# Second attention of a one-core kernel: narrow products and selection issued in batches of eight instead of four

## The reference

```python
qh = q.reshape(B, h, dq, Lq)     # 32 batches, 8 heads, 8 channels, 256 queries
kh = k.reshape(B, h, dq, Lk)     # 256 keys
vh = v.reshape(B, h, dv, Lk)
qk = jnp.einsum('bhdq,bhdl->bhql', qh, kh) * scale
sm = jax.nn.softmax(qk, axis=-1)
ret = jnp.einsum('bhql,bhdl->bhdq', sm, vh)
```

## Time and profile before

| what | value |
|---|---|
| median of 3 runs | 817.76 us |
| profiled execution, first to last instruction (span) | 814.5 us |
| TensorE busy | 755.2 us (93%) |
| VectorE busy | 513.3 us (63%) |
| ScalarE busy | 435.3 us (53%) |
| stage of the change, from the first st to the last `products` | about 270.9 to 520.2 us |
| mean granted TensorE clock | 0.975 |

### The profile page before, as it was taken

How to read it: one execution, slowest core, us unless ns; L and a number is a source line. 1 busy time by engine, 2 the same in 40 slices (tenths; PEclk the granted TensorE clock), 3 DMA queues, 4 the chain that set the end, 5 groups by cost and what they waited for, 6 DMA issues and landing times. The chain is left out here.

```text
span 814.5 us, 16953 instructions
## 1 busy us (share of the span) xinstructions
PE 755.2 (93%) x5377; PEld 576.9 (71%) x5377; DVE 513.3 (63%) x871; ACT 435.3 (53%) x862; POOL 295.0 (36%) x354
## 2 busy tenths in 40 slices
PE   4788889999995999999999999689999999999997
PEld 3677667888985666666666666367787778878776
DVE  3888857897797877887788787462344244253222
ACT  3888834344442777778777787633322332233221
POOL 3455542224446524433533443153222223213222
PEclk9999979999996899999999999889999999999999
DMA  5444410000004433433333331000000000000000
GB/s 146 119 112 128 116 59 1 1 0 0 1 21 127 131 99 97 113 109 94 110 106 100 94 112 44 1 1 1 1 1 27 1 1 26 0 0 0 27 1 27
DMA packets 48093, 43.88 MB, mean 54 GB/s; under 512 B 7860, under 2 KB 46356, under 8 KB 48052
## 3 DMA queue, kind: packets, MB, share of 16 engines
q1 hardware_dynamic: 45892, 37.46, 16.2%
q0 software_dynamic: 2160, 5.90, 2.6%
HBM read 27.99 MB, written 15.07 MB: 53 GB/s over the span
## 5 line engine op out<-in xcount | busy, mean ns | idle before, releaser
L1321 DVE TENSOR_REDUCE a_smax<-a_s 128x4 f32<-128x1024 f32 x128 | 154.4, 1209 | 46.6 <-PE a_s L1255 46.4
L1155 ACT ACTIVATE a_prob<-a_st 128x512 f32<-128x512 f32 x256 | 144.6, 591 | 34.9 <-PE a_st L1243 33.8
L1593 POOL TENSOR_TENSOR f_hs_lo<-f_hid,f_hs_hi 128x512 fp32r<-128x512 f32 (+1 forms) x56 | 73.3, 1308 | 197.4 <-ACT f_hs_hi L1539 197.4
L1243 PE MATMUL a_st<-qop,kop 128*128 128x256 f32 x512 | 120.7, 318 | 1.0 <-DMA qop<-a_neg_t 0.6
L1243 PEld LDWEIGHTS a_st<-qop,kop 128*128 128x128 f32 x512 | 77.2, 189 | 60.3 <-ACT a_prob L1155 44.2
L117 PE MATMUL f_bank<-wd_hi,f_hs_hi 128*128 128x256 f32 (+1 forms) x352 | 104.4, 297 | 7.2 <-POOL f_hs_lo L800 6.2
L1653 DVE TENSOR_TENSOR f_prod<-f_sg,f_bank 128x512 f32<-128x512 f32 x44 | 30.2, 687 | 128.1 <-PE f_bank L119 110.4
L1539 ACT ACTIVATE f_hs_hi<-f_hid 128x512 fp32r<-128x512 f32 (+1 forms) x56 | 35.4, 632 | 139.4 <-PE f_bank L119 99.8
L1255 PE MATMUL a_s<-kop,qop 127*128 127x256 f32 x512 | 104.9, 291 | 4.9 <-DVE a_smax L1321 2.6
L119 PE MATMUL f_bank<-wd_hi,f_hs_lo 128*128 128x256 f32 (+1 forms) x352 | 99.3, 282 | 0.0
L118 PE MATMUL f_bank<-wd_lo,f_hs_hi 128*128 128x256 f32 (+1 forms) x352 | 99.0, 281 | 0.0
(11 more groups left out here) (180 smaller groups left out, 1393.0 us busy)
## 6 DMA issues: line engine op xcount, KB each, us to landing
kop<-kop_rows SPq DMA_DIRECT2D x128, 48.0 KB
qop<-qop_rows SPq DMA_DIRECT2D x128, 48.0 KB
kop_rows<-k_hi SPq DMA_DIRECT2D x32, 128.0 KB, 2.3
qop_rows<-q_hi POOLq DMA_DIRECT2D x30, 128.0 KB, 2.6
x_all<-in_x SPq DMA_DIRECT2D x4, 512.0 KB, 4.7
ctx_t<-in_ctx SPq DMA_DIRECT2D x16, 128.0 KB, 2.0
kop_rows<-k_lo SPq DMA_DIRECT2D x16, 128.0 KB, 2.3
a_ctx<-in_ctx SPq DMA_DIRECT2D x16, 128.0 KB, 2.1
```

What stands on the lines that cost most here:

```text
L1155: act.activation(prob[:, u % 8], st_ps[u % 2][:], ACT.Exp, scale=SCALE1).then_inc(prob_ready, 1)
L1243: mm = pe.matmul(st_ps[u % 2][:, c * D:(c + 1) * D], lhsT=kop[t.slot][:, u // 4, c * P:(c + 1) * P], rhs=qop[t.slot][:, u // 4, u % 4], st ...
L1321: dve.tensor_reduce(smax[:, v.slot, 2 * j:2 * j + 2].rearrange("p u q -> p (u q)"), s_ps[j % 2][:].rearrange("p u (q n) -> p (u q) n", q=2 ...
L1593: pool.tensor_tensor(hs[1][0:r, c % 2], hid[0:r, c % 2], raw(hs[0][0:r, c % 2]), ALU.subtract).then_inc(hs_ready, 1)
```

## The change

`products` loses its argument c and issues both halves of the keys in one go, which makes eight products in place of four, or 16 instructions. `selected` likewise loses m and issues both parts together. The places in the unit loop change with it: the last quad of tile o at u = 2, behind `turn`, in place of u = 1 and 3; the first three quads of tile t at u = 6, 10 and 14 in place of 5 and 7, 9 and 11, 13 and 15; the selection at u = 7 in place of 6 and 8. The waits are the same ones, ahead of the whole batch. The number of products and what they compute stay as they are, and no other engine's program changes.

```diff
--- before.py
+++ after.py
@@ -1196,38 +1196,36 @@
                             mm = pe.transpose(misc[0:HALF, q * P:(q + 1) * P], raw(neg[:, h, q]), ident[:])
                         mm.then_inc(neg_done, 1)
 
-                def products(w_, q, c):
+                def products(w_, q):
 
                     if not w_.inside(TILES):
                         return
-                    if c == 0:
-                        after(pe, prob_ready, w_, UNITS, 4 * q + 4)
-                        after(pe, vt_ready, w_)
-                        if q:
-                            after(pe, pv_ready, w_, QUADS, q)
-                        else:
-                            after(pe, pv_ready, w_.plus(-1), QUADS)
-                    for v4 in range(4):
-                        u = 4 * q + v4
-                        mm = pe.matmul(pv_ps[v4 * 32:(v4 + 1) * 32, 0:D], lhsT=vt[:, w_.slot, c, u],
-                                       rhs=prob[:, u % 8, c * D:(c + 1) * D], start=(c == 0), stop=(c == DC - 1),
-                                       tile_position=(0, v4 * 32))
-                    if c == DC - 1:
-                        mm.then_inc(pv_done, 1)
-
-                def selected(w_, m):
+                    after(pe, prob_ready, w_, UNITS, 4 * q + 4)
+                    after(pe, vt_ready, w_)
+                    if q:
+                        after(pe, pv_ready, w_, QUADS, q)
+                    else:
+                        after(pe, pv_ready, w_.plus(-1), QUADS)
+                    for c in range(DC):
+                        for v4 in range(4):
+                            u = 4 * q + v4
+                            mm = pe.matmul(pv_ps[v4 * 32:(v4 + 1) * 32, 0:D], lhsT=vt[:, w_.slot, c, u],
+                                           rhs=prob[:, u % 8, c * D:(c + 1) * D], start=(c == 0), stop=(c == DC - 1),
+                                           tile_position=(0, v4 * 32))
+                    mm.then_inc(pv_done, 1)
+
+                def selected(w_):
 
                     if not w_.inside(TILES):
                         return
-                    if m == 0:
-                        after(pe, pv_ready, w_, QUADS)
-                        if t.inside(TILES):
-                            after(pe, neg_t_ready, t, 2)
-                    for q in range(QUADS):
-                        mm = pe.matmul(misc[q * 32:(q + 1) * 32, m * D:(m + 1) * D], lhsT=(sel_out, sel_den)[m][:],
-                                       rhs=pv[:, w_.slot, q], start=True, stop=True, tile_position=(0, q * 32))
-                    if m == 1:
-                        mm.then_inc(sel_done, 1)
+                    after(pe, pv_ready, w_, QUADS)
+                    if t.inside(TILES):
+                        after(pe, neg_t_ready, t, 2)
+                    for m in range(2):
+                        for q in range(QUADS):
+                            mm = pe.matmul(misc[q * 32:(q + 1) * 32, m * D:(m + 1) * D], lhsT=(sel_out, sel_den)[m][:],
+                                           rhs=pv[:, w_.slot, q], start=True, stop=True, tile_position=(0, q * 32))
+                    mm.then_inc(sel_done, 1)
 
                 for u in range(UNITS):
                     j, k = divmod(u, 2)
@@ -1258,12 +1256,12 @@
                             mm.then_inc(s_done, 1)
                     if u == 2:
                         turn(t, 1, lambda: after(pe, vt_ready, t))
-                    if u in (1, 3):
-                        products(o, 3, u // 2)
-                    if u % 2 and u > 3:
-                        products(t, u // 4 - 1, u % 4 // 2)
-                    if u in (6, 8):
-                        selected(o, u // 2 - 3)
+                    if u == 2:
+                        products(o, 3)
+                    if u in (6, 10, 14):
+                        products(t, (u - 6) // 4)
+                    if u == 7:
+                        selected(o)
                     if u == 11:
                         def before():
                             after(pe, neg_t_ready, t, 2)
```

## The result

The changed kernel takes 825.99 us (median of 4 runs, 824.92 to 827.43) against 817.76 before: a ratio of 1.0102, 95% interval 1.0086 to 1.0119. It is slower by 8.2 us where 10.3 were forecast. Its profiled execution has a span of 824.4 us, for which the sum had said 824.8.

What follows compares the result with a forecast made beforehand. TensorE's own order bounds the kernel: a 15.83 us step less 1.67 saved, plus 0.05 for `turn` and 2.21 of waits, gives 16.42. With both end tiles that adds 10.3 us to 817.8, so 828 us, range 811 to 834.

Steps and rivals of the forecast that it cites:

- the sum: Whole stage: 8.3 us from fourteen full steps, 0.5 from the first tile, 1.5 from the last, 10.3 slower in all.
- TensorE's order as the bound before: Kernel before: TensorE's own order fills the 15.83 us step; ScalarE and VectorE have some 3 us of slack.
- The saving of a merge: TensorE's batches: each merged pair saves 0.33 us, five pairs a step save 1.67 us.
- The waits for the exponential: Runs between batches: st waits for ScalarE's exponential of two units before, delays of 0.50, 0.23, 0.64 and 0.67 us.
- The walk: One changed step followed with durations from the earlier trace: 2.21 us of waits, a 16.42 us step; chance 0.66.
- The loop of 1.19 us: Two st buffers: from a run's first st through its exponential to the third st's weight load takes 1.19 us.
- One sign that the prediction named: Changed trace: st weight loads wait for exponentials at units 5, 6, 10, 14, 1 and 2, 0.25 to 0.6 us each.
- The late `turn`: Unit 2: VectorE's negation lets `turn` go at 2.74 where TensorE comes at 2.57, a delay of 0.17 us.
- The end of the stage: Last tile, without s: exponentials hold it more, four units take 3.4 us; +1.5 us, between 0 and 2.5.
- Rival 1: Faster: the exponentials' loop doesn't close and batches cover the rest; 793 us without waits, 809 at the lower bound; chance 0.14.
- Rival 2: No change: waits without bare loads or late `turn`, 1.34 us a step; 815.3 to 820.2 us; chance 0.10.
- Rival 3: VectorE takes over: bunched reductions make s wait in two runs, 0.3 us each; 836 us; chance 0.10.

Runs made afterwards that it cites:

- half reductions: Changed kernel with each VectorE maximum over 128 of the 256 keys: 824.15 us, ratio 1.0083 against the kernel before.
- half exponentials: Changed kernel with ScalarE's exponentials over 256 of the 512 columns: 821.18 us, ratio 1.0045 against the kernel before.
- moved copies: Changed kernel with ScalarE's quad copies one unit earlier: all four 822.81 us, ratio 1.0077; three of them 822.30 us, ratio 1.0063, against the kernel before.

## Why the prediction was right

**TensorE's order as the bound before: right.** Halving both other engines' work moved the kernel before by 0.07% (interval 0.9983 to 1.0003).

**The saving of a merge, 0.33 us: right.** One merge gave 0.33, two 0.65. The Trainium skill's rule that a change of the tiling mode drains the TensorE (TensorEngine Tiling (Array Packing), Tiling Modes, Key Properties) agrees in sign; that the whole 0.33 us is this drain was not tried.

**The waits for the exponential: right in kind, place and nearly in size.** The walk had units 3 to 6 last 3.61 us and units 8 to 10 2.86, from the first st of the run to the first st of the next; the trace has 3.63 and 2.86. In units 11 to 14 the walk had st 14 at 2.27 behind st 11; it is at 2.25 in one step and at 2.19 in the next. In units 15 to 2 it had st 1 at 1.35 and st 2 at 2.09; they are at 1.30 and 2.06. A step came to 16.19 for 16.42, which makes the waits 16.19 - 14.21 = 1.98 us for 2.21. The loop of 1.19 us, found in the first tile, is the 1.20 of units 3 to 5 after the change. Two spacings of the walk, 0.48 and 0.49 behind an exponential, don't follow from the lines of the earlier trace rows to which it points, but the trace before has them: its exponential at 362.37 is followed by the copy at 362.86.

One sign that the prediction named doesn't tell the kernels apart: weight loads of st that wait for an exponential are as frequent in the kernel before (see the half reductions).

**The late `turn`, 0.17: wrong.** The walk let TensorE come to `turn` 2.57 us behind the first st of the run and the negation release it at 2.74. Its products start at 2.64, which is 0.58 behind st 2 and the pace without a wait: 0.34 behind a bare load and 0.24, where the walk had counted 0.48. With half reductions, where the negation ends 0.7 us earlier, they start at 2.64 as well. The negation took 0.34 or 0.35 us in this place, not the 0.52 of the earlier trace rows. But the margin is next to nothing: the weight load of `turn` starts 0.12 behind the negation's end, at 2.57 in one step and at 2.63 in the next. So as soon as the waits for ScalarE shrink, by half exponentials or by moved copies, s and `turn` wait for VectorE, and `turn` the more as the negation, beside GpSimd's addition, then takes 0.52 to 0.57.

**The sum: two errors that cancel in part.** Counted as the sum counts, from the first st of a tile, the first tile gave 0.4 us for 0.5, the 14 full steps 5.0 for 8.3, and the last tile 2.7 for 1.5. A full step grew by 0.36 us where the walk had 0.59. The end of the stage was undersized: four units in the last tile take the 3.4 us that the walk said, but its distance to before was cut down to 1.5 where the trace has 2.7 (first st of the tile to the last batch: 512.25 to 527.83 after, 506.27 to 519.15 before).

**The rivals.** Rival 1 (no wait, pure gain) is what the two halved engines give in part, 0.90 of 1.6 us a step; in the kernel as it is ScalarE's waits stand, and VectorE's behind them. Rival 2 is refused by the interval. Rival 3, VectorE in charge, is refused for the changed kernel by the halved reductions, and is what comes right behind. No branch of the forecast had that: rival 1 let the loop of the exponentials open and left VectorE out, but with half exponentials alone the step was still 15.80 us. The chance given to "faster" would have needed both to vanish.

## What to carry to other kernels

A merge that saves time on the busiest engine also takes away the gaps in which the others caught up. Before merging, take from the trace how long a double buffer's loop is (here 1.19 us from one st to the second next) and how much work fits between: merge as long as the runs left between batches don't exceed it. Here two units fit between two batches, so two merges of five brought 1.05%, and all five cost 1.0%; a run of three lost 0.23 to 0.30 us, about what one merge brings. Where a run is one unit too long, move independent work of the same engine into it; tried once here, it brought 0.14 us a step. And look at what stands next in line before shortening a wait: here it was VectorE's negation, which ended with an instruction of a third engine.

## What was not expected of the hardware

VectorE's negation of 128x16 numbers, always the same instruction, lasted from 0.17 to 0.77 us in the changed kernel's trace. The traces show what goes with it: of the 448 negations in the 14 traces, 334 end 0.03 to 0.05 us behind the end of a GpSimd instruction that ran beside them, 100 last 0.17 or 0.18 us, and the other 14 last 0.22 to 0.46. The 0.52 us of the earlier trace rows is one of the first kind; GpSimd's addition beside it lasts from 364.55 to 365.28, and the negation ends at 365.32. No run was made to test what sets it.

A page of the Trainium skill warns that short idle times of the TensorE between groups of matmuls let its clock gate swing between the levels (TensorE: Matmul & The Clock Gate, A second HAM failure mode: psum-queue depth-cycling). In the changed kernel TensorE was idle for 0.4 us in a step of 16.17, and its weight loads of st stood idle until an exponential some seven times in a step, for up to 0.5 us. The granted clock stayed at 1.00, 2.4 GHz, throughout these steps.
